# Second attention: the last two key tiles of exponentials summed on DVE instead of PE

## Chip, core and metric

The kernel runs on one core of a Trainium2 chip. The metric is the device time of one execution in microseconds (us); of several executions the median counts.

## What is computed

A convolutional attention, then a token attention, then routed experts, on eight images of 256 channels and 32x32 = 1024 tokens. The change lies in the token attention (the second attention):

```python
qk = jnp.einsum('bhqd,bhkd->bhqk', q, k)
qe = jnp.einsum('bhqd,qkd->bhqk', q, embeddings)
weights = jax.nn.softmax((qk + qe) / jnp.sqrt(jnp.float32(d_head)), axis=-1)
output = jnp.einsum('bhqk,bhkd->bhqd', weights, v)
```

There are 8 heads of 32 channels. The kernel computes the softmax as exponentials, a product of the unnormalized exponentials with the values, and a division by the sum of the exponentials (the denominator).

## The kernel before

The second attention is `attention_keys_first`. One **unit** of its work is one image, one group of four heads and one half (512) of the queries: 8 x 2 x 2 = 32 units. Keys lie on the partitions, so a unit has `KTU` = 8 **tiles** of 128 keys, and a tile has four exponential blocks of 128x512 f32, one for each head. The exponentials of the last `PR` = 4 tiles are kept in the ring `prob`. `prob`, the running sums `acc`, the reciprocals `rec` (and in the changed kernel `pair`) all are slices of one buffer that the trace calls `bias`.

The order of work is written out by hand: a loop over n = 8u + kt on each engine. I call the passage for one n a **step**, and number the steps of a unit 0 to 7 by `n % KTU`.

- **PE**, step n: the scores of heads 0 and 1 of tile n (`scores`, L1264), two products of a later unit's search for row extremes (`maxima`, L1145), the scores of heads 2 and 3, then `weigh(n-1)` (L1284), the product of tile n-1's exponentials with the values. Score s may start when exponential s-2 has been made (two PSUM buffers). The two products of `maxima` have one PSUM buffer each; each may start when DVE has read what stood in its buffer (`max_read`).
- **ACT**, step n: four exponentials (L1338), one a head. Before the first of a tile it waits until the ring's place is free: until tile n-4 has been weighed (`weighed`) and summed (`acc_ok`). In step 1 it also copies the unit's output from PSUM (L1323).
- **POOL** sums tiles 0 to 5 of a unit into `acc`: `ADDS` = 5 instructions of 128x2048 f32 (L1366), each after all four exponentials of its tile. After the fourth it normalizes the unit before (`finish`, L1349 and L1353), which needs that unit's four reciprocals, and then it makes the fifth sum.
- **DVE**, step n: reads the two products of `maxima` (L1153, 128x1024 from PSUM, 1 out); in steps 3 to 6 also one of the four reciprocals (L1381) of the unit before.
- **Denominators.** PE multiplies by a matrix of ones (`den_w`) and accumulates three groups of four matmuls in `den_ps`: the exponentials of tile 6 and of tile 7, each straight from `prob`, behind their `weigh` (L1293, in step 7 and in step 0 of the next unit), and Pool's sum `acc` in step 2 of the next unit (`denominators`, L1300).

Of the kernel before, what the change touches and what calls it, by code (L numbers as in the profile page):

```python
# [6 lines left out]
def build(nc, x, gamma, wqkv, wout, w1q, b1cols, b1v, gatew, experts, relt, cw0, cb0, cw1, cb1, cw2, cb2,  # L7
# [3 lines left out]
    ALU = mybir.AluOpType  # L11
# [7 lines left out]
    H, D = 8, C // 8  # L19
    G = H * D // P  # L20
    HG = H // G
# [9 lines left out]
    CH = 512  # L31
# [22 lines left out]
    with ctx:  # L54
# [1003 lines left out]
        def attention_keys_first():  # L1058
            with ExitStack() as es:
# [3 lines left out]
                def tile(name, shape, dt):  # L1063
                    return es.enter_context(nc.sbuf_tensor(f"{name}_kf", shape, dt))
# [11 lines left out]
                prob = zf[:, 0:o1].rearrange("p (r j n) -> p r j n", r=PR, j=HG)  # L1076
                acc = zf[:, o1:o2].rearrange("p (r j n) -> p r j n", r=2, j=HG)
                rec = zf[:, o2:o2 + 2 * CH].rearrange("p (r n) -> p r n", r=2)
                oS = tile("oS", [P, 2, CH], F32)
                oN = tile("oN", [P, CH], F32)  # L1080
                den_w = tile("den_w", [P, D], F32)
# [17 lines left out]

                sems = [ssem(n) for n in ("stk0", "stk1", "v_in0", "v_in1", "x_in0", "x_in1", "out_st0", "out_st1", "m_in0",  # L1100
                                          "m_in1", "emb_in", "fill", "max_full", "max_read", "full", "exps", "weighed",
                                          "acc_ok", "den", "recd", "taken", "scaled", "fin")]
                (stk0, stk1, v_in0, v_in1, x_in0, x_in1, out_st0, out_st1, m_in0, m_in1, emb_in, fill, max_full, max_read,
                 full, exps, weighed, acc_ok, den, recd, taken, scaled, fin) = sems
                stk, v_in, x_in, out_st, m_in = (stk0, stk1), (v_in0, v_in1), (x_in0, x_in1), (out_st0, out_st1), (m_in0, m_in1)

                def load_group(sp, q, b, g):
# [110 lines left out]
                with nc.Fori(0, B // NB) as i_:  # L1218
                    with nc.Block() as block:
# [35 lines left out]
                        def _(pe):  # L1255
# [19 lines left out]
                            def weigh(n):  # L1275
                                u, kt = divmod(n, KTU)
                                g, bb = (u // NC) % G, u // UB
                                if kt == 0 and u % UB == 0 and bb >= 1:
                                    pe.wait_ge(v_in[bb % 2], 16 * ((bb + 1) // 2))
                                if kt == 0 and u >= 1:  # L1280
                                    pe.wait_ge(taken, u)
                                pe.wait_ge(exps, HG * (n + 1))
                                for j in range(HG):
                                    last = nc.tensor.matmul(out_ps[j * D:(j + 1) * D, :],  # L1284
                                                            V[:, bb % 2, kt, (g * HG + j) * D:(g * HG + j + 1) * D],
                                                            prob[:, n % PR, j, :], start=(kt == 0), stop=(kt == KTU - 1),
                                                            skip_group_check=True)
                                if kt > ADDS:

                                    if kt == ADDS + 1 and u >= 1:  # L1290
                                        pe.wait_ge(recd, PIECES * u)
                                    for j in range(HG):
                                        last = nc.tensor.matmul(den_ps[j * D:(j + 1) * D, :], den_w[:], prob[:, n % PR, j, :],  # L1293
                                                                start=(kt == ADDS + 1), stop=False, skip_group_check=True)
                                last.then_inc(weighed, 1)

                            def denominators(u):
                                pe.wait_ge(acc_ok, ADDS * (u + 1))
                                for j in range(HG):
                                    last = nc.tensor.matmul(den_ps[j * D:(j + 1) * D, :], den_w[:], acc[:, u % 2, j, :],  # L1300
                                                            start=False, stop=True, skip_group_check=True)
                                last.then_inc(den, 1)

                            for n in range(NU * KTU + DEN + 1):
# [12 lines left out]
                        def _(act):  # L1317
# [7 lines left out]
                            for s in range(NS_ + SU):  # L1325
# [5 lines left out]
                                if n >= PR and j == 0:  # L1331

                                    u, kt = divmod(n - PR, KTU)
                                    act.wait_ge(weighed, n - PR + 1)
                                    if kt <= ADDS:
                                        act.wait_ge(acc_ok, ADDS * u + max(kt, 1))
                                act.wait_ge(full, s + 1)
                                nc.scalar.activation(prob[:, n % PR, j, :], score_ps[s % 2], ACT.Exp,  # L1338
                                                     scale=-1.0 / (W1S * W1S)).then_inc(exps, 1)
# [35 lines left out]
                        def _(dve):  # L1375
                            def reciprocal(u, piece):
# [3 lines left out]
                                c = slice(piece * CH // PIECES, (piece + 1) * CH // PIECES)  # L1380
                                nc.vector.reciprocal(rec[:, u % 2, c], den_ps[:, c]).then_inc(recd, 1)  # L1381

                            for n in range(NU * KTU + REC + PIECES):
                                if n < NU * KTU:
                                    for u, m in step_jobs[n]:
                                        max_reduce(dve, job_at[(u, m)], u, m)
                                u, piece = n // KTU - 1, n % KTU - REC
                                if u >= 0 and 0 <= piece < PIECES:
                                    reciprocal(u, piece)
# [503 lines left out]
```

## Time and profile before

| | us |
|---|---|
| median of 3 runs | 2957.65 |
| lowest, highest | 2957.21, 2963.11 |
| profiled execution, its own time | 2944.62 |
| its span in the trace | 2942.8 |
| busy PE, DVE, POOL, ACT | 2554.9, 2020.5, 1972.1, 1399.7 |
| matmuls of the second attention's scores (L1264), busy | 531.8 |
| Pool's sums of the second attention (L1366), busy | 724.8 |

The span is what the trace covers; the profiled execution's own time is 1.8 us longer and is one of the shorter ones seen. Busy times of PE count overlapping matmuls once for each stretch, so neighbouring groups of matmuls are best read by the distance between their starts. A time line row gives the start, the length of the merged group, the engine, the line, and in brackets how long the engine was idle before it and what released it.

### The profile page before, as it was taken

Reading aid. Unit: us, or ns where it says so; the run is one execution under the profiler, and the core shown is the slowest. Engines: PE = TensorE matmul, PEld = TensorE weight load, DVE = VectorE, ACT = ScalarE, POOL = GpSimd, SP = SyncE. Lnnn points to the kernel's source line nnn. Section 1 sums busy time; section 2 is a strip of 40 time slices with the busy share of each in tenths; the row PEclk is TensorE's granted clock in tenths of the full one; section 3 lists DMA queues with packets and bytes.
Section 4 is the critical chain, followed back from the end, with each engine's and each line's share of the span. In section 5 each row is a group of like instructions: output and inputs, shape, how many; then the busy total and the mean of one; then the engine's idle time right before and its main releaser. Section 6 shows DMA issues by size and latency. Waiting matters only on the chain. (4 is left out here: it accounts for less than half of the span.)

```text
span 2942.8 us, 47730 instructions
## 1 busy us (share of the span) xinstructions
PE 2554.9 (87%) x18726; PEld 871.1 (30%) x18726; DVE 2020.5 (69%) x3094; ACT 1399.7 (48%) x2549; POOL 1972.1 (67%) x767
## 2 busy tenths in 40 slices
PE   5669999999999999969998999999999999870355
PEld 1436222222222222225553222222222222250235
DVE  3346678787787878757776777777777777668224
ACT  3224555556555555523224555555555555450012
POOL 0312688888888888864445888878888788750673
PEclk8789999999999999989999999999999999985558
DMA  2985232122312223229654233222232222180237
GB/s 51 214 228 180 69 77 61 52 48 52 86 48 51 48 62 76 51 95 285 232 203 138 48 81 75 61 48 62 79 76 62 47 62 72 36 259 0 83 120 257
DMA packets 239569, 289.44 MB, mean 98 GB/s; under 512 B 65014, under 2 KB 172790, under 8 KB 236006
## 3 DMA queue, kind: packets, MB, share of 16 engines
q1 hardware_dynamic: 196528, 259.08, 31.9%
q0 software_dynamic: 6144, 16.85, 1.8%
q10 hardware_dynamic: 36672, 10.45, 1.6%
q8 instruction: 148, 2.42, 0.4%
q14 instruction: 77, 0.63, 0.1%
HBM read 176.55 MB, written 111.57 MB: 98 GB/s over the span
## 5 line engine op out<-in xcount | busy, mean ns | idle before, releaser
L1018 POOL TENSOR_TENSOR room_af<-room_af 128x2048 f32<-128x2048 f32 x160 | 726.9, 4543 | 162.6 <-ACT room_af L990 148.9
L1366 POOL TENSOR_TENSOR bias<-bias 128x2048 f32<-128x2048 f32 x160 | 724.8, 4530 | 147.6 <-ACT bias L1338 133.6
L1153 DVE TENSOR_REDUCE row_min_kf<-PS 128x1 f32<-128x1024 f32 x532 | 627.5, 1220 | 265.8 <-PE PS L1145 264.3
L797 DVE CUSTOM_DVE_ANT_0 PS<-PS,bias 128x1024 f32<-128x1024 f32 x532 | 644.3, 1241 | 174.6 <-PE PS L785 148.3
L1338 ACT ACTIVATE bias<-PS 128x512 f32<-128x512 f32 x1024 | 557.0, 596 | 411.0 <-PE PS L1264 409.9
L990 ACT ACTIVATE room_af<-PS 128x512 f32<-128x512 f32 x1024 | 555.9, 594 | 398.0 <-PE PS L912 398.0
L1264 PE MATMUL PS<-stacks_kf 128*128 128x512 f16 x2048 | 531.8, 382 | 7.5 <-PEq L85 7.1
L905 PE MATMUL PS<-QS_af,KS_af 128*128 128x512 f16 x1024 | 334.1, 387 | 11.1 <-PEq L85 4.5
L1264 PEld LDWEIGHTS PS<-stacks_kf 128*128 128x128 f16 x2048 | 157.0, 97 | 446.8 <-ACT bias L1338 291.6
L938 PE MATMUL PS<-room_af,V_af 128*32 128x512 f32 x2048 | 272.7, 605 | 0.3 <-ACT room_af L990 0.3
L1284 PE MATMUL PS<-bias,V_kf 128*32 128x512 f32 x2048 | 272.7, 604 | 0.0
L912 PE MATMUL PS<-turned_bias,eyes 64*32 64x512 f16 x4096 | 210.6, 388 | 0.0
L785 PE MATMUL PS<-KM_af,QM_af 32*128 32x512 f16 x1064 | 133.9, 386 | 52.5 <-DVE row_min_af L797 32.8
L1145 PE MATMUL PS<-stacks_kf 64*128 64x512 f16 x1064 | 168.8, 383 | 1.6
L905 PEld LDWEIGHTS PS<-QS_af,KS_af 128*128 128x128 f16 x1024 | 70.7, 97 | 306.0 <-ACT room_af L990 231.0
L1693 POOL DMA_INDIRECT G_t<-token_rows,idxT_t x64 | 65.9, 1029 | 109.5 <-DVE valT_t L1808 90.3
L577 POOL TENSOR_TENSOR room_af<-room_af 128x1024 f16<-128x1024 f32 x16 | 34.0, 2126 | 149.8 <-ACT room_af L535 149.7
L1381 DVE RECIPROCAL bias<-PS 128x128 f32<-128x128 f32 x128 | 121.0, 947 | 6.0 <-PE PS L1300 6.0
L470 PE MATMUL PS<-xh,w_p 128*128 128x512 f16 x384 | 124.4, 383 | 0.0
L1037 DVE RECIPROCAL room_af<-room_af 128x128 f32<-128x128 f32 x128 | 121.1, 948 | 1.1
L1664 ACT CAST gh_t<-PS 128x256 f16<-128x256 f32 x64 | 23.8, 373 | 202.4 <-PE PS L1594 202.1
L912 PEld LDWEIGHTS PS<-turned_bias,eyes 64*32 64x32 f16 x4096 | 57.4, 89 | 186.3 <-issue 186.3
(179 smaller groups left out, 2844.7 us busy)
## 6 DMA issues: line engine op xcount, KB each, us to landing
stacks_kf<-query_key_halves SPq DMA_DIRECT2D x119, 256.0 KB, 7.2
query_key_halves<-bias SPq DMA_DIRECT2D x32, 768.0 KB, 3.8
query_key_halves<-room_af SPq DMA_DIRECT2D x32, 512.0 KB, 3.0
KS_af<-query_key_halves SPq DMA_DIRECT2D x51, 256.0 KB, 4.8
QS_af<-query_key_halves SPq DMA_DIRECT2D x51, 256.0 KB, 7.0
V_kf<-values SPq DMA_DIRECT2D x9, 1024.0 KB, 10.8
V_af<-values SPq DMA_DIRECT2D x17, 512.0 KB, 8.8
stacks_kf<-query_key_halves SPq DMA_DIRECT2D x68, 128.0 KB, 9.4
```

Of the source, the lines that this page charges most:

```text
L797: nc.vector.tensor_tensor_reduce(out=max_ps[n % len(max_ps)], in0=max_ps[n % len(max_ps)], in1=bias[:, g * HG + j, z:z + N], scale=-1.0, s ...
L905: nc.tensor.matmul(score_ps[s % 3], KS[:, g, j, kt * P:(kt + 1) * P], QS_[:, g, j, first:first + CH], start=True, stop=False, skip_group_c ...
L912: last = nc.tensor.matmul(score_ps[(HG * n + 2 * pair + i) % 3][c * W:(c + 1) * W, :], eyes[half, :], turned_bias[half, 2 * g + pair, z:z ...
L938: last = nc.tensor.matmul(out_ps[j * D:(j + 1) * D, :], V[:, q % 2, kt, j * D:(j + 1) * D], prob[:, n % PR, j, :], start=(kt == 0), stop=( ...
L990: nc.scalar.activation(prob[:, n % PR, head, :], score_ps[s % 3], ACT.Exp).then_inc(exps, 1)
L1018: nc.gpsimd.tensor_tensor(acc[:, u % 2], so_far, prob[:, n % PR], ALU.add).then_inc(acc_ok, 1)
L1145: last = nc.tensor.matmul(max_ps[n % len(max_ps)][:, c * CH:(c + 1) * CH], stacks[half, slot, QHH, j, first + t * P:first + (t + 1) * P], ...
L1153: nc.vector.tensor_reduce(row_min[:, m:m + 1], max_ps[n % len(max_ps)], AX.X, ALU.min).then_inc(max_read, 1)
L1264: last = nc.tensor.matmul(score_ps[s % 2], stacks[:, slot, k_, j, kt * P:(kt + 1) * P], stacks[:, slot, q_, j, first:first + CH], start=(n ...
L1284: last = nc.tensor.matmul(out_ps[j * D:(j + 1) * D, :], V[:, bb % 2, kt, (g * HG + j) * D:(g * HG + j + 1) * D], prob[:, n % PR, j, :], st ...
L1338: nc.scalar.activation(prob[:, n % PR, j, :], score_ps[s % 2], ACT.Exp, scale=-1.0 / (W1S * W1S)).then_inc(exps, 1)
L1366: nc.gpsimd.tensor_tensor(acc[:, u % 2], so_far, prob[:, n % PR], ALU.add).then_inc(acc_ok, 1)
```

## The change

PE no longer multiplies tiles 6 and 7 by `den_w` one after the other. DVE adds the two tiles, head by head, into a new buffer `pair`: four `tensor_tensor` instructions of 128x512 f32 (`add_pair`), two in step 0 and two in step 1 of the next unit, each behind one of the two reads of `maxima` in that step. `denominators`, still in step 2 of the next unit, now issues two groups of four matmuls, one from `pair` and one from `acc`. PE waits there for `paired`, for `acc_ok` and for the reciprocals of the unit before. ACT, before it writes over tiles 6 and 7 in the ring (at the start of steps 2 and 3 of the next unit), now waits for `paired` too.

```diff
--- before.py
+++ after.py
@@ -1076,6 +1076,7 @@
                 prob = zf[:, 0:o1].rearrange("p (r j n) -> p r j n", r=PR, j=HG)
                 acc = zf[:, o1:o2].rearrange("p (r j n) -> p r j n", r=2, j=HG)
                 rec = zf[:, o2:o2 + 2 * CH].rearrange("p (r n) -> p r n", r=2)
+                pair = zf[:, o2 + 2 * CH:o2 + 6 * CH].rearrange("p (j n) -> p j n", j=HG)
                 oS = tile("oS", [P, 2, CH], F32)
                 oN = tile("oN", [P, CH], F32)
                 den_w = tile("den_w", [P, D], F32)
@@ -1099,9 +1100,9 @@
 
                 sems = [ssem(n) for n in ("stk0", "stk1", "v_in0", "v_in1", "x_in0", "x_in1", "out_st0", "out_st1", "m_in0",
                                           "m_in1", "emb_in", "fill", "max_full", "max_read", "full", "exps", "weighed",
-                                          "acc_ok", "den", "recd", "taken", "scaled", "fin")]
+                                          "acc_ok", "paired", "den", "recd", "taken", "scaled", "fin")]
                 (stk0, stk1, v_in0, v_in1, x_in0, x_in1, out_st0, out_st1, m_in0, m_in1, emb_in, fill, max_full, max_read,
-                 full, exps, weighed, acc_ok, den, recd, taken, scaled, fin) = sems
+                 full, exps, weighed, acc_ok, paired, den, recd, taken, scaled, fin) = sems
                 stk, v_in, x_in, out_st, m_in = (stk0, stk1), (v_in0, v_in1), (x_in0, x_in1), (out_st0, out_st1), (m_in0, m_in1)
 
                 def load_group(sp, q, b, g):
@@ -1285,20 +1286,17 @@
                                                             V[:, bb % 2, kt, (g * HG + j) * D:(g * HG + j + 1) * D],
                                                             prob[:, n % PR, j, :], start=(kt == 0), stop=(kt == KTU - 1),
                                                             skip_group_check=True)
-                                if kt > ADDS:
-
-                                    if kt == ADDS + 1 and u >= 1:
-                                        pe.wait_ge(recd, PIECES * u)
+                                last.then_inc(weighed, 1)
+
+                            def denominators(u):
+                                if u >= 1:
+                                    pe.wait_ge(recd, PIECES * u)
+                                pe.wait_ge(paired, HG * (u + 1))
+                                pe.wait_ge(acc_ok, ADDS * (u + 1))
+                                for i, part in enumerate((pair, acc[:, u % 2])):
                                     for j in range(HG):
-                                        last = nc.tensor.matmul(den_ps[j * D:(j + 1) * D, :], den_w[:], prob[:, n % PR, j, :],
-                                                                start=(kt == ADDS + 1), stop=False, skip_group_check=True)
-                                last.then_inc(weighed, 1)
-
-                            def denominators(u):
-                                pe.wait_ge(acc_ok, ADDS * (u + 1))
-                                for j in range(HG):
-                                    last = nc.tensor.matmul(den_ps[j * D:(j + 1) * D, :], den_w[:], acc[:, u % 2, j, :],
-                                                            start=False, stop=True, skip_group_check=True)
+                                        last = nc.tensor.matmul(den_ps[j * D:(j + 1) * D, :], den_w[:], part[:, j, :],
+                                                                start=(i == 0), stop=(i == 1), skip_group_check=True)
                                 last.then_inc(den, 1)
 
                             for n in range(NU * KTU + DEN + 1):
@@ -1334,6 +1332,8 @@
                                     act.wait_ge(weighed, n - PR + 1)
                                     if kt <= ADDS:
                                         act.wait_ge(acc_ok, ADDS * u + max(kt, 1))
+                                    else:
+                                        act.wait_ge(paired, HG * (u + 1))
                                 act.wait_ge(full, s + 1)
                                 nc.scalar.activation(prob[:, n % PR, j, :], score_ps[s % 2], ACT.Exp,
                                                      scale=-1.0 / (W1S * W1S)).then_inc(exps, 1)
@@ -1380,10 +1380,24 @@
                                 c = slice(piece * CH // PIECES, (piece + 1) * CH // PIECES)
                                 nc.vector.reciprocal(rec[:, u % 2, c], den_ps[:, c]).then_inc(recd, 1)
 
+                            def add_pair(u, j):
+                                dve.wait_ge(exps, HG * KTU * (u + 1))
+                                if u >= 1:
+                                    dve.wait_ge(den, u)
+                                last = KTU * (u + 1) - 1
+                                nc.vector.tensor_tensor(pair[:, j, :], prob[:, (last - 1) % PR, j, :], prob[:, last % PR, j, :],
+                                                        ALU.add).then_inc(paired, 1)
+
                             for n in range(NU * KTU + REC + PIECES):
+                                u, kt = n // KTU - 1, n % KTU
+                                heads = [2 * kt, 2 * kt + 1] if u >= 0 and kt < HG // 2 else []
                                 if n < NU * KTU:
-                                    for u, m in step_jobs[n]:
-                                        max_reduce(dve, job_at[(u, m)], u, m)
+                                    for u_, m in step_jobs[n]:
+                                        max_reduce(dve, job_at[(u_, m)], u_, m)
+                                        if heads and m < MH:
+                                            add_pair(u, heads.pop(0))
+                                for j in heads:
+                                    add_pair(u, j)
                                 u, piece = n // KTU - 1, n % KTU - REC
                                 if u >= 0 and 0 <= piece < PIECES:
                                     reciprocal(u, piece)
```

How it moves the instructions. On **DVE**, from step 6 of a unit (the row of L1155 or L1156 is the transposed extremes) to the first reciprocal of the next unit, before:

```order
L1155 TENSOR_SCALAR max_row_kf<-PS 16x128 [waits max_full_kf]
L1153 TENSOR_REDUCE row_min_kf<-PS 128x1 [waits max_full_kf] x2
L1381 RECIPROCAL bias<-PS 128x128 [waits den_kf]
L1153 TENSOR_REDUCE row_min_kf<-PS 128x1 [waits max_full_kf] x10
L1381 RECIPROCAL bias<-PS 128x128 [waits den_kf]
L1153 TENSOR_REDUCE row_min_kf<-PS 128x1 [waits max_full_kf] x2
L1381 RECIPROCAL bias<-PS 128x128 [waits den_kf]
L1153 TENSOR_REDUCE row_min_kf<-PS 128x1 [waits max_full_kf] x2
L1381 RECIPROCAL bias<-PS 128x128 [waits den_kf]
```

and now, from the same place (L1388 is `add_pair`; `bias` is the common buffer):

```order
L1156 TENSOR_SCALAR max_row_kf<-PS 16x128 [waits max_full_kf]
L1154 TENSOR_REDUCE row_min_kf<-PS 128x1 [waits max_full_kf] x2
L1381 RECIPROCAL bias<-PS 128x128 [waits den_kf]
L1154 TENSOR_REDUCE row_min_kf<-PS 128x1 [waits max_full_kf] x3
L1388 TENSOR_TENSOR bias<-bias 128x512 [waits den_kf,exps_kf]
L1154 TENSOR_REDUCE row_min_kf<-PS 128x1 [waits max_full_kf]
L1388 TENSOR_TENSOR bias<-bias 128x512 [waits den_kf,exps_kf]
L1154 TENSOR_REDUCE row_min_kf<-PS 128x1 [waits max_full_kf]
L1388 TENSOR_TENSOR bias<-bias 128x512 [waits den_kf,exps_kf]
L1154 TENSOR_REDUCE row_min_kf<-PS 128x1 [waits max_full_kf]
L1388 TENSOR_TENSOR bias<-bias 128x512 [waits den_kf,exps_kf]
L1154 TENSOR_REDUCE row_min_kf<-PS 128x1 [waits max_full_kf] x4
```

Four additions stand between five reads; they wait for the exponentials and, for the buffer `pair`, for the denominators of the unit before. No other DVE instruction of the second attention has changed its place.

On **PE**, the end of step 2, where `denominators` stands behind `weigh`, before:

```order
L1284 MATMUL PS<-bias,V_kf 32x512 [waits exps_kf]
L1284 MATMUL PS<-bias,V_kf 32x512 x3
L1300 MATMUL PS<-bias,den_w_kf 32x512 [waits acc_ok_kf]
L1300 MATMUL PS<-bias,den_w_kf 32x512 x3
L1264 MATMUL PS<-stacks_kf 128x512 [waits exps_kf]
```

and now:

```order
L1285 MATMUL PS<-bias,V_kf 32x512 [waits exps_kf]
L1285 MATMUL PS<-bias,V_kf 32x512 x3
L1298 MATMUL PS<-bias,den_w_kf 32x512 [waits acc_ok_kf,paired_kf,recd_kf]
L1298 MATMUL PS<-bias,den_w_kf 32x512 x7
L1265 MATMUL PS<-stacks_kf 128x512 [waits exps_kf]
```

The group of four has become eight, with two more waits; the groups of L1293 in steps 7 and 0 are gone.

On **ACT**, from the middle of step 1 into step 2, before:

```order
L1338 ACTIVATE bias<-PS 128x512 [waits full_kf,acc_ok_kf,weighed_kf]
L1338 ACTIVATE bias<-PS 128x512 [waits full_kf]
L1323 COPY oS_kf<-PS 128x512 [waits weighed_kf]
L1338 ACTIVATE bias<-PS 128x512 [waits full_kf] x2
L1338 ACTIVATE bias<-PS 128x512 [waits full_kf,weighed_kf]
L1338 ACTIVATE bias<-PS 128x512 [waits full_kf] x3
```

and now:

```order
L1338 ACTIVATE bias<-PS 128x512 [waits full_kf,acc_ok_kf,weighed_kf]
L1338 ACTIVATE bias<-PS 128x512 [waits full_kf]
L1321 COPY oS_kf<-PS 128x512 [waits weighed_kf]
L1338 ACTIVATE bias<-PS 128x512 [waits full_kf] x2
L1338 ACTIVATE bias<-PS 128x512 [waits full_kf,paired_kf,weighed_kf]
L1338 ACTIVATE bias<-PS 128x512 [waits full_kf] x3
```

The first exponential of step 2 has one more wait, `paired_kf`; so has that of step 3.

## Rows read from the trace of the kernel before

**Rows 1.** The page: span, and busy time of each engine.

```profile
span 2942.8 us, 47730 instructions
...
PE 2554.9 (87%) x18726; PEld 871.1 (30%) x18726; DVE 2020.5 (69%) x3094; ACT 1399.7 (48%) x2549; POOL 1972.1 (67%) x767
```

**Rows 2.** Windows: us, then busy PE, PEld, DVE, ACT, POOL, clock, DMA share, GB/s.

```profile
1620.00:2540.00 920.00, 918.41 (x5548) 240.39 (x5548) 677.54 (x630) 532.38 (x990) 753.90 (x210) 1.00 0.26 64
```

**Rows 3.** Groups by line: busy us, mean ns of one, idle before and its releaser.

```profile
L1366 POOL TENSOR_TENSOR bias<-bias 128x2048 f32<-128x2048 f32 x160 | 724.8, 4530 | 147.6 <-ACT bias L1338 133.6 <-POOL bias L1366 0.4
...
L1153 DVE TENSOR_REDUCE row_min_kf<-PS 128x1 f32<-128x1024 f32 x532 | 627.5, 1220 | 265.8 <-PE PS L1145 264.3
...
L1264 PE MATMUL PS<-stacks_kf 128*128 128x512 f16 x2048 | 531.8, 382 | 7.5 <-PEq L85 7.1 <-ACT bias L1338 0.3
...
L1284 PE MATMUL PS<-bias,V_kf 128*32 128x512 f32 x2048 | 272.7, 604 | 0.0
...
L1293 PE MATMUL PS<-bias,den_w_kf 128*32 128x512 f32 x512 | 66.6, 592 | 0.0
...
L1300 PE MATMUL PS<-bias,den_w_kf 128*32 128x512 f32 x256 | 33.7, 597 | 2.2 <-POOL bias L1366 2.2
```

**Rows 4.** Time line of one unit of the second attention (step 0 starts at 1729.62).

```profile
1698.32 4.53 POOL L1366 TENSOR_TENSOR bias<-bias 128x2048 f32<-128x2048 f32 x1
...
1721.48 1.04 PE L1264 MATMUL PS<-stacks_kf 128*128 128x512 f16 x4
...
1726.36 1.27 POOL L1349 TENSOR_TENSOR oN_kf<-oS_kf,bias 128x512 f32<-128x512 f32 x1 [1.19 <-DVE bias L1381]
...
1729.00 4.53 POOL L1366 TENSOR_TENSOR bias<-bias 128x2048 f32<-128x2048 f32 x1
...
1729.62 1.04 PE L1264 MATMUL PS<-stacks_kf 128*128 128x512 f16 x4
...
1731.02 2.35 DVE L1153 TENSOR_REDUCE row_min_kf<-PS 128x1 f32<-128x1024 f32 x2 [1.97 <-PE PS L1145]
...
1733.95 1.04 PE L1264 MATMUL PS<-stacks_kf 128*128 128x512 f16 x4
...
1734.67 1.08 ACT L1338 ACTIVATE bias<-PS 128x512 f32<-128x512 f32 x2 [1.82 <-PE PS L1264]
...
1734.92 0.60 PE L1145 MATMUL PS<-stacks_kf 64*128 64x512 f16 x4
...
1735.46 1.04 PE L1264 MATMUL PS<-stacks_kf 128*128 128x512 f16 x4
...
1736.11 1.12 ACT L1338 ACTIVATE bias<-PS 128x512 f32<-128x512 f32 x2
...
1737.30 4.54 POOL L1366 TENSOR_TENSOR bias<-bias 128x2048 f32<-128x2048 f32 x1 [3.77 <-ACT bias L1338]
...
1737.42 1.04 PE L1264 MATMUL PS<-stacks_kf 128*128 128x512 f16 x4
```

**Rows 5.** The line L1748 alone: shortest, median and longest in ns.

```profile
L1748 DVE TENSOR_SCALAR gates<-lg_t x16: 180/559/1094, 2590.2 to 2643.8; 128x32 f32<-128x32 f32 x16
```

**Rows 6.** Time line of the expert stage, where L1748 meets Pool's L1687.

```profile
2603.82 2.27 POOL L1687 TENSOR_TENSOR xl_t<-bias,xh_t 128x512 f16<-128x512 f32 x2 [1.69 <-ACT xh_t L1634]
...
2604.02 1.00 DVE L1748 TENSOR_SCALAR gates<-lg_t 128x32 f32<-128x32 f32 x1
...
2604.93 0.68 DVE L1755 SCALAR_TENSOR_TENSOR bias<-PS,bias 128x512 f16<-128x512 f32 x1
...
2622.34 0.18 DVE L1748 TENSOR_SCALAR gates<-lg_t 128x32 f32<-128x32 f32 x1
...
2622.49 2.27 POOL L1687 TENSOR_TENSOR xl_t<-bias,xh_t 128x512 f16<-128x512 f32 x2 [1.74 <-ACT xh_t L1634]
```

**Rows 7.** DVE groups by form, f32 from SBUF to SBUF: two inputs, one input.

```profile
L1775 DVE TENSOR_TENSOR gates<-gates,rcp_t 128x512 f32<-128x512 f32 x8 | 5.5, 692 | 0.3
...
L252 DVE TENSOR_SCALAR set_weights<-set_weights 128x768 f32<-128x768 f32 x2 | 1.1, 602 | 0.0
```

More of the change, by code:

```diff
@@ L1287, in weigh @@
                                                             skip_group_check=True)
-                                if kt > ADDS:
-                                    if kt == ADDS + 1 and u >= 1:
-                                        pe.wait_ge(recd, PIECES * u)
-                                    for j in range(HG):
-                                        last = nc.tensor.matmul(den_ps[j * D:(j + 1) * D, :], den_w[:], prob[:, n % PR, j, :],
-                                                                start=(kt == ADDS + 1), stop=False, skip_group_check=True)
                                 last.then_inc(weighed, 1)
                             def denominators(u):
+                                if u >= 1:
+                                    pe.wait_ge(recd, PIECES * u)
+                                pe.wait_ge(paired, HG * (u + 1))
                                 pe.wait_ge(acc_ok, ADDS * (u + 1))
-                                for j in range(HG):
-                                    last = nc.tensor.matmul(den_ps[j * D:(j + 1) * D, :], den_w[:], acc[:, u % 2, j, :],
-                                                            start=False, stop=True, skip_group_check=True)
+                                for i, part in enumerate((pair, acc[:, u % 2])):
+                                    for j in range(HG):
+                                        last = nc.tensor.matmul(den_ps[j * D:(j + 1) * D, :], den_w[:], part[:, j, :],
+                                                                start=(i == 0), stop=(i == 1), skip_group_check=True)
                                 last.then_inc(den, 1)
```

## The prediction

> **What bounds the kernel now.** I read the page first, for the engine that is busiest, then the windows of the second attention, then its groups by line, and last one unit of it in the time line. PE is busy 2554.9 of 2942.8 us [rows 1], and between 1620 and 2540 us it is busy 918.4 of 920 us at a granted clock of 1.00, so at its upper level of 2.4 GHz [rows 2]. DVE is busy 677.5 us there and POOL 753.9. By shares, then, PE is the bound, and DVE has 242 us to spare. The groups say the same: before the scores (L1264) PE has idled 7.5 us in all, and Pool has held PE back by 2.2 us at L1300; DVE waits 264.3 us for products, and Pool 133.6 us for exponentials [rows 3].
>
> The share does not say what a unit's chain of waits tolerates; that needs the time line [rows 4]. Step 0 starts at 1729.62, step 1 at 1733.95, step 2 at 1737.42: a step with a denominator group takes 4.33 us, one without 3.47, so a group of four matmuls costs 0.86 us. A unit takes 30.68 us (Pool's fifth sum starts at 1698.32 and 1729.00). Counted from the start of a step: the first product of L1145 starts at 0.97, the third score at 1.51 (so the second product at about 1.24), the first exponential at 0.72 and the last one ends at 3.28, DVE's two reads start at 1.40 and take 1.18 each.
>
> Two things are nearer to PE than its 99.8% shows. Pool's fifth sum ends at 1733.53, and ACT, which must wait for it before the exponentials of step 1, starts them at 1734.67: 1.1 us of slack. And two exponentials are made in 1.08 us; the first of them ends 1.26 us into a step, 0.25 us before the third score that waits for it starts. A late exponential reaches PE after about 0.15 us (0.25 less some 0.1 for the signal, my estimate).
>
> **What the change takes away.** Two groups before (steps 7 and 0), one more in step 2: one group of 0.86 us a unit, 32 x 0.86 = 27.5 us, all of it on PE. Steps 7 and 0 shrink to 3.47, step 2 grows from 4.33 to 5.2. A unit would take 29.82 us if nothing else held it.
>
> **What it adds.** Four additions a unit on DVE, 128x512 f32, two inputs in SBUF. The same form took 692 ns in the routing [rows 7], 0.65 from start to start if successive instructions overlap by 0.04 as the reads do (1220 ns each, 1.18 apart). That is 4 x 0.65 x 32 = 83 us, which DVE's spare time covers by share. What matters is when they run, and beside what.
>
> *When.* All times now count from step 0. Pool's fifth sum hangs on the reciprocals of step 6: it starts 7.52 us after step 6 does (1721.48, [rows 4]), through `finish`, which waited for DVE 1.19 us. Step 0 used to come 8.14 us after step 6, now 7.28. So the sum runs from 0.24 to 4.77, while the exponentials of step 1 are due at 3.47 + 0.72 = 4.19: the slack of 1.1 us has turned into 0.6 late. With additions that nothing hinders, DVE does read 1.40 to 2.58, addition to 3.23, read to 4.41, addition to 5.06, and in step 1 read, addition, read, addition to 8.72. ACT now waits for that last addition before step 2's exponentials, due at 6.94 + 0.72 = 7.66. So they are 1.1 late, PE loses 0.95 (this contains the 0.6), and a unit takes 29.82 + 0.95 = 30.8 instead of 30.68. Even undisturbed, the whole gain is given back.
>
> *Beside what.* The trace shows that some DVE instructions and Pool's exclude each other. L1748, a DVE instruction of 32 elements, takes between 180 and 1094 ns, median 559 [rows 5]. At 2622.34 no Pool instruction runs yet: 0.18 us. At 2604.02 the first of two Pool subtractions (2603.82, 2.27 us for both, so the first ends near 2604.97) is under way: 1.00 us, ending at 2605.02, so it waited out that instruction and got in ahead of the second one [rows 6]. The neighbour that reads PSUM (L1755) took its 0.68 with Pool beside it, and the 532 reads of L1153 average 1220 ns under Pool's sums. L1748 has one input, in SBUF; the rows show that such f32 instructions go at double rate (768 elements in 602 ns, where two inputs need 692 for 512, [rows 7]), hence through two read paths. An addition of two SBUF tensors needs two read paths as well, so I take it that it too waits for a Pool instruction under way, and holds up the next. No row shows a two-input addition beside Pool; that is the open step. The bounds are 0.65 for an addition (nothing held) and 4.53 + 0.65 = 5.2 (a whole sum of L1366 waited for, [rows 3]).
>
> The Trainium skill, "SBUF — State Buffer", section "Who interferes with whom", says that a DVE instruction with two SBUF inputs contends with a GpSimd instruction that reads SBUF, and that the pair of ports goes to whoever starts first, for the whole instruction. By that rule the additions behave as I assume; without it the sum would be the 30.8 us above. The trace agrees for the one-input form (0.18 against 1.00 us), and shows neither for the two-input one.
>
> **The sum with exclusion.** DVE's first addition is ready at 2.58, Pool's sum runs until 4.77: it ends at 5.42, the second read at 6.60. PE's second product of step 1, due at 3.47 + 1.24 = 4.71, waits for that buffer: **1.9 us lost**, queued behind it the two later scores. The second addition finds Pool idle and ends at 7.25, the read at 8.43. The exponentials of tile 1 end at 3.47 + 3.28 + 1.9 = 8.65, and Pool's first sum could start at 8.72; the third addition is there 0.3 us earlier and takes 8.43 to 9.08. Pool's sum runs 9.08 to 13.61. DVE's read ends at 10.26, and the fourth addition waits for Pool: 13.61 to 14.26. ACT may start step 2's exponentials at 14.3, where 6.94 + 0.72 + 1.9 = 9.56 was due: 4.75 late, **4.6 us lost** on PE (a product of step 2 that waits until 10.26 is inside that). From there Pool has nothing that meets an addition, the reciprocals keep their place, and the next fifth sum again ends 4.77 after step 0. A unit takes 29.82 + 6.5 = 36.3 us, 5.6 more than 30.68. Over the 31 units behind the first: 175 us. The last unit pays some 2 us (its additions meet the last sum; one group less on PE). Together 177: the profiled execution's 2944.6 would become 3122. The median of the runs shown is 13 us above that execution, so I give 2957.65 + 177 = **3135**.
>
> **The rivals.**
> - *Pool gets in first.* The lead of the third addition is only 0.3 us. If Pool's first sum starts at 8.72, the additions end at 13.90 and 15.73, step 2 loses 6.05 and a unit 7.95 + 29.82 = 37.8: 7.1 more, 222 in all, **3180**. For it: the lead is small beside signals that I estimate at 0.1. Against it: the chain from the second read runs over PE, ACT (two exponentials, 1.12) and Pool, against an addition and a read, 1.83 us.
> - *Sharing instead of exclusion.* If the two only slow each other (additions twice as long beside Pool, the sum longer by 0.65), the fourth ends near 10.1, ACT is 2.5 late, a unit takes 1.5 more: +47, **3005**. Against it: in rows 6 the short instruction ended with Pool's, not after a share of it.
> - *Nothing held: the two-input form is not affected.* 30.8 a unit, +3 to +5: **2961**, within 0.2%, which is about what a measurement here can tell from no change. For it: only the one-input form is seen waiting.
> - *Faster.* Neither wait binds: PE takes the full 27.5 us, **2930**. It needs the fourth addition done by about 7.8, so additions of 0.43 us, and nothing held. A form that takes 692 ns speaks against it; it turns into a gain over 0.2% once an unhindered unit loses under 0.65 us of the 0.86 instead of 0.95, which exponentials with 0.3 us more slack would give.
>
> **How the numbers follow.** Forecast 0.58, Pool first 0.22, sharing 0.07, nothing held 0.09, faster 0.04. The forecast's own ends: if a held addition has read its inputs before and ends 0.25 after Pool instead of 0.65, two of them give back 0.8 us a unit, 25 us: 3110; signals of 0.2 where I took 0.1 add 10. With Pool first and the same allowance the upper end is 3195, the lower one 3100; this leaves out the last three cases, 0.20. Slower holds 0.58 + 0.22 + 0.07 and a sliver of "nothing held": 0.88; within 0.2%, 0.08; faster 0.04.
>
> **What would show it.** Right: the first and fourth additions of a unit last about 2.9 and 4 us and start while L1366 runs, the second and third about 0.7; L1145 and the exponentials of step 2 gain idle time released by DVE, some 2 and 5 us a unit; units 36.3 us apart; PE's busy share of the stage falls to about 82% at a clock that stays 1.00; the groups before and behind the stage are unchanged. Pool first: the third addition is long as well. Wrong: four additions of 0.7 us each beside L1366, and units of 30.8 us. A granted clock below 1.00 in the stage would add time that I have not counted.

## The result and the profile after

| | before | after |
|---|---|---|
| median, us | 2957.43 | 3170.22 |
| lowest to highest, us | 2956.62 to 2963.11 | 3167.54 to 3175.49 |
| profiled execution, its own time | 2944.62 | 3175.49 |

The changed kernel is slower: ratio 1.0717, 95% interval 1.0698 to 1.0736, 213 us. The forecast was 3135, the range 3100 to 3195.

The page of the kernel after, span and busy times, to be read against [rows 1]:

```profile
span 3173.7 us, 47502 instructions
...
PE 2594.9 (82%) x18470; PEld 875.8 (28%) x18470; DVE 2260.6 (71%) x3222; ACT 1402.9 (44%) x2549; POOL 1971.6 (62%) x767
```

PE is busy 40 us more, although its matmul instructions are 256 fewer (18470 against 18726); DVE is busy 240 us more, where four additions a unit, unhindered, are 83. The windows after, of the second attention and of two stretches of one of its units (columns as in [rows 2]):

```profile
1620.00:2740.00 1120.00, 950.31 (x5288) 242.11 (x5288) 894.06 (x746) 534.34 (x987) 749.07 (x209) 0.95 0.21 52
...
1772.90:1775.70 2.80, 2.76 (x12) 0.63 (x16) 1.57 (x2) 1.61 (x3) 0.91 (x1) 0.67 0.00 0
1775.70:1778.30 2.60, 2.60 (x20) 0.52 (x12) 0.00 (x0) 0.00 (x0) 2.60 (x1) 0.70 0.00 0
```

Before, PE was busy 99.8% of the stage at a clock of 1.00; now it is busy 84.8% at 0.95. The groups by line after (lines 1145, 1264 and 1284 of before are now 1146, 1265 and 1285; against [rows 3]):

```profile
L1338 ACT ACTIVATE bias<-PS 128x512 f32<-128x512 f32 x1024 | 557.0, 595 | 619.5 <-PE PS L1265 407.9 <-DVE bias L1388 161.9 <-POOL bias L1366 49.5
...
L1265 PE MATMUL PS<-stacks_kf 128*128 128x512 f16 x2048 | 536.2, 384 | 133.4 <-ACT bias L1338 126.2 <-PEq L85 7.1
...
L1388 DVE TENSOR_TENSOR bias<-bias 128x512 f32<-128x512 f32 x128 | 252.1, 1972 | 0.0
...
L1146 PE MATMUL PS<-stacks_kf 64*128 64x512 f16 x1064 | 174.1, 384 | 52.0 <-DVE row_min_kf L1154 50.3
```

L1265 has idled 133.4 us where it was 7.5, nearly all of it for exponentials; L1146, the products for the extremes, 52.0 us for DVE's reads. ACT in turn waited 161.9 us for the additions and 49.5 for Pool. The additions alone (shortest, median, longest in ns):

```profile
L1388 DVE TENSOR_TENSOR bias<-bias x128: 672/683/4983, 1611.0 to 2778.4; 128x512 f32<-128x512 f32 x128
```

Half of them take 0.68 us, the longest 5 us, and their mean is 1972 ns. The time line of one unit shows which (against [rows 4]):

```profile
1758.51 1.04 PE L1265 MATMUL PS<-stacks_kf 128*128 128x512 f16 x4
1758.76 4.52 POOL L1366 TENSOR_TENSOR bias<-bias 128x2048 f32<-128x2048 f32 x1
...
1761.05 2.78 DVE L1388 TENSOR_TENSOR bias<-bias 128x512 f32<-128x512 f32 x1
...
1761.98 1.04 PE L1265 MATMUL PS<-stacks_kf 128*128 128x512 f16 x4
...
1764.89 0.67 DVE L1388 TENSOR_TENSOR bias<-bias 128x512 f32<-128x512 f32 x1
...
1765.02 0.39 PE L1146 MATMUL PS<-stacks_kf 64*128 64x512 f16 x2 [1.68 <-DVE row_min_kf L1154]
...
1766.62 0.67 DVE L1388 TENSOR_TENSOR bias<-bias 128x512 f32<-128x512 f32 x1
1767.15 4.51 POOL L1366 TENSOR_TENSOR bias<-bias 128x2048 f32<-128x2048 f32 x1 [3.87 <-ACT bias L1338]
...
1767.31 1.04 PE L1265 MATMUL PS<-stacks_kf 128*128 128x512 f16 x4
...
1768.36 3.85 DVE L1388 TENSOR_TENSOR bias<-bias 128x512 f32<-128x512 f32 x1
...
1772.29 1.08 ACT L1338 ACTIVATE bias<-PS 128x512 f32<-128x512 f32 x2 [5.22 <-DVE bias L1388]
...
1772.94 1.14 PE L1265 MATMUL PS<-stacks_kf 128*128 128x512 f16 x4 [4.06 <-ACT bias L1338]
...
1778.32 1.04 PE L1265 MATMUL PS<-stacks_kf 128*128 128x512 f16 x4
...
1796.02 1.04 PE L1265 MATMUL PS<-stacks_kf 128*128 128x512 f16 x4
```

Step 0 starts at 1758.51. The first addition starts at 1761.05, while Pool's fifth sum runs (1758.76 to 1763.28), and ends at 1763.83; the second takes 0.67. The second product of step 1 waits 1.68 us for a read behind them. The third addition comes 0.53 us before Pool's first sum; the fourth starts 1.2 us into that sum (1767.15 to 1771.66) and ends at 1772.21. ACT starts step 2's exponentials at 1772.29, and PE, idle for 4.06 us, takes up the third score at 1772.94. From there to step 3 it needs 5.38 us, where the schedule has 3.47 - 1.51 + 2 x 0.86 = 3.68: the windows above show a granted clock of 0.67 and 0.70, that is, part of the time at 1.2 GHz.

The unit's account: step 1 lasts 5.33 us instead of 3.47 (**1.86 lost**); the third score of step 2 comes 5.63 us into the step instead of 1.51 (**4.12 lost**); the rest of step 2 takes 5.38 instead of 3.68 (**1.70 lost, the clock**). 29.82 + 7.68 = 37.5, which is what lies between 1758.51 and 1796.02. Over 30 units the mean is 37.56, against 30.70 before; 31 x 6.86 = 213 us, the whole difference. Nothing outside the second attention is needed to explain it. (The two profiled executions differ by more, 231 us. Of these, 212 lie between the first and the last row of L1155/L1156, 2 ahead of it and 16 behind it. From that last row to the end of the trace before takes 391 us and after 408; the other traces below take 393 to 411 there, and the kernel before with nothing but Pool's order changed takes 402. So the 16 us are the spread of that stage from one execution to the next, and not the change.)

### The profile page after: what moved, and what is told of

Read it like the earlier page. It is cut to its first block and busy times, and to the rows that moved or that the text cites. A ratio compares the mean times of both kernels' runs of the same rounds, so it can differ in the third digit from the quotient of the medians.

```text
span 3173.7 us, 47502 instructions
## 1 busy us (share of the span) xinstructions
PE 2594.9 (82%) x18470; PEld 875.8 (28%) x18470; DVE 2260.6 (71%) x3222; ACT 1402.9 (44%) x2549; POOL 1971.6 (62%) x767
## 5 line engine op out<-in xcount | busy, mean ns | idle before, releaser
L1265 PE MATMUL PS<-stacks_kf 128*128 128x512 f16 x2048 | 536.2, 384 | 133.4 <-ACT bias L1338 126.2
L1265 PEld LDWEIGHTS PS<-stacks_kf 128*128 128x128 f16 x2048 | 155.2, 97 | 568.0 <-ACT bias L1338 424.9
L1285 PE MATMUL PS<-bias,V_kf 128*32 128x512 f32 x2048 | 299.5, 660 | 0.0
L1388 DVE TENSOR_TENSOR bias<-bias 128x512 f32<-128x512 f32 x128 | 252.1, 1972 | 0.0
L1146 PE MATMUL PS<-stacks_kf 64*128 64x512 f16 x1064 | 174.1, 384 | 52.0 <-DVE row_min_kf L1154 50.3
L1622 PE MATMUL PS<-bias,gh_t 128*128 128x256 f16 x256 | 62.6, 344 | 88.9 <-DVE gl_t L1831 68.4
```

The costliest lines, as they stand in the source:

```text
L1265: last = nc.tensor.matmul(score_ps[s % 2], stacks[:, slot, k_, j, kt * P:(kt + 1) * P], stacks[:, slot, q_, j, first:first + CH], start=(n ...
L1285: last = nc.tensor.matmul(out_ps[j * D:(j + 1) * D, :], V[:, bb % 2, kt, (g * HG + j) * D:(g * HG + j + 1) * D], prob[:, n % PR, j, :], st ...
L1388: nc.vector.tensor_tensor(pair[:, j, :], prob[:, (last - 1) % PR, j, :], prob[:, last % PR, j, :], ALU.add).then_inc(paired, 1)
```

## The experiments

All ratios are against the kernel before, timed on the same chip beside them (2947.18 us for the first four, 2962.81 for the next four, 2958.73 for the last three). "Unit" is the mean distance between the rows of L1155/L1156, over 30 units of the trace.

**One operand from PSUM.** 

```diff
+ other = den_ps if u >= 1 else prob[:, last % PR, j, :]
- nc.vector.tensor_tensor(pair[:, j, :], prob[:, (last - 1) % PR, j, :], prob[:, last % PR, j, :], ALU.add)
+ nc.vector.tensor_tensor(pair[:, j, :], prob[:, (last - 1) % PR, j, :], other, ALU.min)
```

> The addition of each head takes its second operand from PSUM (the denominators' bank) and not from SBUF, as a minimum; place, length and waits stay, the sum over tile 7 is left out. Theory (an instruction of DVE with two SBUF inputs and one of Pool's exclude each other): nothing is held, all four last about 0.7 us, a unit takes 30.8 us, time about 2961. Rival (any DVE instruction that reads the buffer that Pool reads is held): first and fourth still last 2.8 and 3.9 us, time stays near 3170.

2952.16 us, ratio 1.0018 (1.0008 to 1.0027), unit 30.61. Its lines of the additions:

```profile
L1389 DVE TENSOR_TENSOR bias<-bias,PS x124: 674/677/682, 1645.7 to 2563.3; 128x512 f32<-128x512 f32 x124
L1389 DVE TENSOR_TENSOR bias<-bias x4: 681/683/4130, 1610.0 to 1615.2; 128x512 f32<-128x512 f32 x4
```

124 additions with one operand in PSUM stand at the same places, beside the same sums of Pool, read the same buffer, and take 674 to 682 ns. The four of the first unit, which kept both operands in SBUF, include one of 4130 ns. So what is held is the instruction with a second SBUF input; the buffer and the place do not matter. (The minimum is not what frees it either: the one of 4130 ns is a minimum too.) The run also confirms that the change, with nothing held, gives nearly its whole gain back: 0.77 of 0.86 us a unit (30.61 against 29.84 in the last run). The 5 us by which the kernel is slower than before are about what its first unit, with that one held addition, takes more than the others (35.69 against 30.60).

**One column.** 

```diff
- pair[:, j, :], prob[:, (last - 1) % PR, j, :], prob[:, last % PR, j, :]
+ pair[:, j, 0:1], prob[:, (last - 1) % PR, j, 0:1], prob[:, last % PR, j, 0:1]
```

> Each addition covers 1 column instead of 512; it still has two SBUF inputs, and all waits stay (the denominators leave out nearly all of tiles 6 and 7). Theory: what costs is the waiting, not the adding. The first still ends with Pool's fifth sum (4.9 us after step 0 starts), the fourth with Pool's first sum (near 12.8). PE loses 1.35 and 3.65 us and 0 to 1.7 us for the clock: units of 34.8 to 36.5 us, time 3085 to 3140. Rival (the 2.7 us of added DVE work hold up the reads): without the work a unit takes 30.3 us, time about 2946.

3158.50 us, ratio 1.0715 (1.0696 to 1.0733), unit 37.50: as slow as the change, and above what I expected. From its time line:

```profile
1791.69 2.25 DVE L1388 TENSOR_TENSOR bias<-bias 128x1 f32<-128x1 f32 x1
...
1797.26 4.50 POOL L1366 TENSOR_TENSOR bias<-bias 128x2048 f32<-128x2048 f32 x1 [3.34 <-ACT bias L1338]
1797.40 4.37 DVE L1388 TENSOR_TENSOR bias<-bias 128x1 f32<-128x1 f32 x1
...
1802.51 1.89 PE L1265 MATMUL PS<-stacks_kf 128*128 128x512 f16 x4 [3.51 <-ACT bias L1338]
...
1808.98 1.04 PE L1265 MATMUL PS<-stacks_kf 128*128 128x512 f16 x4
```

An addition of one column, 0.14 us where it is free, takes 2.25 and 4.37 us: the work is not what costs. PE's idle time fell as expected (1.15 us in step 1, 3.51 in step 2). But from the third score at 1802.51 to step 3 PE took 6.47 us instead of 3.68, and the windows of that stretch (columns as in [rows 2]) show the lower clock all through its first part:

```profile
1802.50:1806.00 3.50, 3.49 (x12) 0.79 (x16) 1.54 (x2) 1.64 (x3) 0.89 (x1) 0.50 0.75 143
1806.00:1808.90 2.90, 2.90 (x20) 0.59 (x12) 0.00 (x0) 0.00 (x0) 2.90 (x1) 0.60 0.00 0
```

So the clock took 2.8 us here and not the 0 to 1.7 I had allowed. That left a question, for the last series.

**No additions.** `add_pair` and the waits for `paired` go; both groups in `denominators` multiply `acc`, so tiles 6 and 7 are left out of the denominators and PE's work stays.

> No additions on DVE and no waits for them; PE multiplies Pool's sum twice, so its two groups of four stay (the denominators leave out tiles 6 and 7). It gives what PE's saved group is worth at best. If PE alone bounds: 29.82 us a unit, time 2930. By my reading of the slack, Pool's fifth sum is now 0.6 us late for step 1's exponentials and takes back 0.5: 30.3 us a unit, time about 2946. In no case above 2957.

2939.74 us, ratio 0.9974 (0.9962 to 0.9986), unit 30.42, where I expected 30.3. Waits of this kernel from 1700 to 2400 us (total, times, longest):

```profile
ACT bias L1335 <- POOL bias L1363: 37.1, 23, 1.6
```

ACT waits 1.6 us a unit for Pool's fifth sum, and the best that the rest of the change could bring as it stands is 7.4 us (2947.18 - 2939.74).

**Pool's sums in halves.** 

```diff
- nc.gpsimd.tensor_tensor(acc[:, u % 2], so_far, prob[:, n % PR], ALU.add).then_inc(acc_ok, 1)
+ for h in range(2):
+     hs = slice(h * HG // 2, (h + 1) * HG // 2)
+     nc.gpsimd.tensor_tensor(acc[:, u % 2, hs], so_far[:, hs], prob[:, n % PR, hs], ALU.add).then_inc(acc_ok, 1)
```

Everyone who waits for `acc_ok` waits for twice the count.

> Pool makes each sum in two instructions of 128x1024 (about 2.35 us each) instead of one of 128x2048. Theory (DVE is held until the Pool instruction under way ends, and then gets in before the next one): no addition is held for longer than 2.3 us, the fourth ends near 11 us after step 0 starts instead of 13.7; PE loses some 3.2 us a unit: 33.0 us, time about 3030, up to 3070 if the clock still falls. Rivals: if two Pool instructions in a row keep the ports, or if the hold is not tied to an instruction's end, the time stays at 3170 or rises, since Pool has 0.15 us more work a sum.

3057.97 us, ratio 1.0367 (1.0347 to 1.0387), unit 34.14, where I expected 33.0 and up to 3070 us if the clock still falls. Time line of Pool's pairs of halves and the two held additions:

```profile
1815.46 5.18 POOL L1368 TENSOR_TENSOR bias<-bias 128x1024 f32<-128x1024 f32 x2
...
1819.48 1.71 DVE L1390 TENSOR_TENSOR bias<-bias 128x512 f32<-128x512 f32 x1
...
1823.35 5.10 POOL L1368 TENSOR_TENSOR bias<-bias 128x1024 f32<-128x1024 f32 x2 [2.71 <-ACT bias L1338]
...
1823.98 2.26 DVE L1390 TENSOR_TENSOR bias<-bias 128x512 f32<-128x512 f32 x1
...
1828.78 4.67 POOL L1368 TENSOR_TENSOR bias<-bias 128x1024 f32<-128x1024 f32 x2 [0.33 <-ACT bias L1338]
```

An undisturbed pair takes 4.67 us; the two pairs with an addition inside take 5.18 and 5.10. The held additions, the second and the fourth of this unit, last 1.71 and 2.26 us, where the change had 2.78 and 3.85. Of the pair at 1823.35 the first half ends at 1825.69, the addition at 1826.24 and the second half at 1828.45. So the hold ends with Pool's instruction, DVE gets in ahead of the next one though that is ready, and then Pool waits for DVE: the exclusion works both ways. The units of this run are not alike: most are near 33.2, 33.9 or 34.8 us. In those of 33.2 PE goes from the third score of step 2 to step 3 in 3.74 us, in those of 34.8 in 5.2 to 5.4; from 1640 to 2500 us the granted clock is 0.97 on average. So part of what lies above the expected 33.0 is again the lower clock.

**Filling PE's wait.** In step 2 of the changed kernel, before the third score:

```diff
+ pe.wait_ge(acc_ok, ADDS * (ud + 1))
+ for _ in range(4):
+     for j in range(HG):
+         nc.tensor.matmul(den_ps[j * D:(j + 1) * D, :], den_w[:], acc[:, ud % 2, j, :], start=True, stop=True, ...)
```

(`ud` is the unit before; a wait for its predecessor's reciprocals is left out here.)

> In step 2, behind the products for the extremes, PE issues four groups of four extra matmuls (the ones matrix by Pool's sum, into the denominators' bank, written over afterwards): 3.45 us of useless work in the 4.06 us in which it otherwise waits for the fourth addition. All waits stay. If the lower granted clock behind that wait costs 1.7 us a unit, a unit falls from 37.5 to 35.8 us: some 52 us less than the change, 160 above before, although PE has 110 us more to do. If the clock is not the cause, the time is that of the change (210 above before) or more.

3132.18 us, ratio 1.0573 (1.0557 to 1.0589), unit 35.92. The window of its stage (columns as in [rows 2]) and the time line of its step 2 (L1314 is the useless work; the trace has two records for one f32 matmul, so x32 are 16 matmuls):

```profile
1640.00:2500.00 860.00, 805.58 (x5007) 210.09 (x5006) 720.53 (x599) 427.21 (x790) 602.05 (x168) 1.00 0.22 55
...
1798.32 3.89 DVE L1397 TENSOR_TENSOR bias<-bias 128x512 f32<-128x512 f32 x1
...
1798.78 3.64 PE L1314 MATMUL PS<-bias,den_w_kf 128*32 128x512 f32 x32
...
1802.95 1.09 PE L1265 MATMUL PS<-stacks_kf 128*128 128x512 f16 x4 [0.53 <-ACT bias L1347]
...
1806.69 1.04 PE L1265 MATMUL PS<-stacks_kf 128*128 128x512 f16 x4
```

The fourth addition is as long as before and ACT resumes as late, yet from the third score to step 3 PE takes 3.74 us and not 5.38. 110 us of additional matmuls make the kernel 1.3% faster (1.0573 against 1.0717), and the granted clock of the stage is 1.00 where the change had 0.95. This shows the 1.7 us a unit to be the clock's.

**Pool's fifth sum first.** Two lines in Pool's loop:

```diff
- if n % KTU == FIN and n >= KTU:
+ if n % KTU == ADDS and n >= KTU:
      finish(n // KTU - 1)
```

(and `finish` waits for the previous `fin`, since two of them now follow one another at the end).

> Pool makes its fifth sum before it normalizes the unit before, not after; the additions stay where they are. The fifth sum then ends 0.6 us before step 0 starts, the normalizing about 2 us after, so Pool is free when the first addition comes (2.6 us): the first, second and third last 0.7 us, PE's loss of 1.9 us in step 1 goes. The fourth still meets Pool's first sum, now from 6.9 to 11.4 us, and ends near 12.0: 4.25 us lost in step 2 and 1.7 for the clock. Unit 34.1 to 35.8 us, 105 to 160 above before. If the loss in step 1 is not Pool's doing, 210 above.

3128.26 us, ratio 1.0560 (1.0543 to 1.0576), unit 36.06. Time line:

```profile
1787.36 1.26 POOL L1355 TENSOR_TENSOR res_kf<-res_kf,oN_kf 128x512 f32<-128x512 f32 x1
...
1789.05 0.68 DVE L1390 TENSOR_TENSOR bias<-bias 128x512 f32<-128x512 f32 x1
...
1792.52 0.68 DVE L1390 TENSOR_TENSOR bias<-bias 128x512 f32<-128x512 f32 x1
...
1793.34 4.50 POOL L1368 TENSOR_TENSOR bias<-bias 128x2048 f32<-128x2048 f32 x1 [4.72 <-ACT bias L1338]
...
1794.25 4.13 DVE L1390 TENSOR_TENSOR bias<-bias 128x512 f32<-128x512 f32 x1
...
1799.12 1.89 PE L1265 MATMUL PS<-stacks_kf 128*128 128x512 f16 x4 [4.09 <-ACT bias L1338]
```

Pool's normalizing ends at 1788.6, the first addition is at 1789.05: three additions of 0.68 (two shown), no loss in step 1. The fourth, 0.9 us behind the start of Pool's first sum, still takes 4.13. The time is a little above what I expected: the wait in step 2 was as expected (4.09 us idle, the third score 4.16 late), which leaves 36.06 - 29.82 - 4.16 = 2.1 us a unit, on average, for the clock. It is not the same in every unit: most are 35.3 and 36.4 us long in turn, behind the same wait. The granted clock from 1640 to 2500 us is 0.93.

**Fifth sum first, and all four additions in step 0.** One before the first read, one behind it, two behind the second:

```diff
- heads = [2 * kt, 2 * kt + 1] if u >= 0 and kt < HG // 2 else []
+ heads = list(range(HG)) if u >= 0 and kt == 0 else []
+ if heads:
+     add_pair(u, heads.pop(0))
```

> As with the fifth sum first, and all four additions stand in step 0: one before the first read, one behind it, two behind the second. All meet only the short normalizing instructions of Pool (1.3 us each) and end near 5.7 us, a microsecond before Pool's first sum can start; the reads end at 8.1 us, in time for step 2. Nothing holds PE: 29.85 us a unit, 26 us below before (0.991). Rival (the DVE work itself delays the reads, or the waits bind anyhow): no gain, 30.7 us or more a unit.

2944.27 us against 2962.81, ratio 0.9930 (0.9917 to 0.9944), unit 30.07 (29.85 expected): **faster than both kernels**, by little, but the whole interval lies below 1. Time line of its step 0 (1789.94) and 1:

```profile
1790.08 1.27 POOL L1351 TENSOR_TENSOR oN_kf<-oS_kf,bias 128x512 f32<-128x512 f32 x1
1790.15 1.75 DVE L1390 TENSOR_TENSOR bias<-bias 128x512 f32<-128x512 f32 x1
...
1791.49 1.54 POOL L1355 TENSOR_TENSOR res_kf<-res_kf,oN_kf 128x512 f32<-128x512 f32 x1
...
1792.96 0.68 DVE L1390 TENSOR_TENSOR bias<-bias 128x512 f32<-128x512 f32 x1
...
1794.39 0.82 PE L1146 MATMUL PS<-stacks_kf 64*128 64x512 f16 x4
1794.69 1.28 DVE L1390 TENSOR_TENSOR bias<-bias 128x512 f32<-128x512 f32 x2
...
1796.95 23.21 POOL L1368 TENSOR_TENSOR bias<-bias 128x2048 f32<-128x2048 f32 x5 [3.92 <-ACT bias L1338]
```

The additions meet only Pool's two normalizing instructions: the first waits for one (1.75 us), and then holds up the other (1.54 instead of 1.28). All four are done at 1795.97, a microsecond before Pool's first sum. The third score of step 1 follows 1.72 us after the step's start (1793.42) instead of 1.51; these 0.21 us are nearly all that lies between 30.07 and the unit of 29.84 that PE's work alone takes (last run).

**The same, but no addition before the first read** (the last two lines of the edit above left out).

> As the run before, but no addition stands before the first read of step 0: one behind the first read, three behind the second and so at the end of step 0. They end near 6.35 us, just ahead of Pool's first sum at 6.8, but the reads of step 1 end 0.5 us later than step 2 wants them: 30.3 to 30.4 us a unit, 9 us below before (0.997). If the fourth misses by half a microsecond and meets Pool's sum, it costs 4 us a unit: 120 above.

2949.46 us, ratio 0.9953 (0.9940 to 0.9967), unit 30.19: also faster than before, its unit 0.1 us longer than the last one's, where I had expected 0.5.

**One column, and the wait filled.** The edits of one column and of filling together (leaving out what the first of them leaves out).

> Additions of one column, and PE fills its wait in step 2 with the four useless groups (3.45 us of the 3.5 it waits). The run with one column alone was as slow as the change (37.53 us a unit) although the fourth addition ended 1.1 us sooner; its trace shows the lower granted clock for 6 us a unit where the change has 3.4. If that is the reason, the clock now stays up and a unit takes what its waits say, 29.82 + 1.33 (step 1) + 3.6 (step 2) = 34.75 us: 126 above before (1.043). If something else ate the gain, 210 above (1.071).

3093.58 us, ratio 1.0454 (1.0437 to 1.0471), unit 34.84. The window of its stage:

```profile
1620.00:2640.00 1020.00, 985.12 (x6137) 255.02 (x6133) 847.87 (x730) 521.30 (x964) 736.56 (x205) 1.00 0.23 57
```

With useless work in the wait the granted clock is 1.00, and the unit is what its waits say. So one column did save 1.1 us of waiting a unit (34.84 against 35.92 with whole additions and the wait filled), and the clock had taken it.

**The kernel before with the fifth sum first.**

> The kernel before, with nothing but Pool's fifth sum made ahead of the normalizing. Pool held nothing up there, so a unit stays at 30.68 us: no difference (1.000). If Pool's order is worth something alone, the gain of the four early additions is not the additions': 0.993.

2958.31 us, ratio 0.9998 (0.9988 to 1.0007), unit 30.70. Pool's order is worth nothing by itself; it only makes room.

**No additions, fifth sum first.** Without the additions, as above.

> No additions and no waits for them, and Pool's fifth sum ahead of the normalizing. The run without additions took 30.41 us a unit where PE's work alone is 29.82; ACT waited for Pool there. If the fifth sum is what is missing, a unit now takes 29.82 us, 27 us below before (0.991). If not, it stays at 30.4 (0.997).

2927.18 us, ratio 0.9888 (0.9872 to 0.9905), unit 29.84. That is PE's own work, 29.82 by the sum.

## Why the prediction was right, and where it was off

The way, the cause and the size of the two waits were right. That the time lies in the range is in part luck: the forecast's own ends were 3110 and 3145, and 3170 is inside only because the range was drawn up to 3195 for Pool coming first, which did not happen.

- *PE's group is worth 0.86 us a unit.* Right: 30.70 - 29.84 where nothing else binds.
- *Pool's fifth sum becomes late by 0.6 us.* Right: without additions a unit took 30.42, and 29.84 with the sum made earlier.
- *Unhindered additions give the gain back: 30.8 us a unit.* Right in kind, 30.61 measured; the signals cost less than I took.
- *Two SBUF inputs and Pool's instruction exclude each other.* This was the open step, inferred from an instruction with one input at double rate [rows 5 to 7]. It held: 2.78 and 3.85 us where I had 2.84 and 4.0, and 0.68 with one operand in PSUM. The Trainium skill ("SBUF — State Buffer", "Who interferes with whom") had the rule for two inputs, and for the PSUM case that an instruction with one SBUF input does not contend (outside DVE's two-port modes); these runs agree with both, 0.68 us against up to 4 us. It speaks of a hold for the whole instruction; Pool's halves agree, since the hold shrank with the instruction.
- *The third addition gets in ahead of Pool's sum.* Right, by 0.53 us where I had 0.3. The rival in which Pool came first, whose 3180 lies nearer to the measured time than my 3135, did not happen: the third addition takes 0.67. A time alone would have chosen the wrong case.
- *PE loses 1.9 and 4.6 us.* 1.86 and 4.12 measured. The fourth addition ended 0.55 us behind Pool's sum, not 0.65, and Pool's sum started 0.4 us sooner, 8.64 us into the unit and not 9.08: I had it wait for the end of the third addition at 9.08, but that ends at 8.78, and the row of Pool's sum starts 0.14 us before that end and is no longer than others (4.51 us).
- *"At a clock that stays 1.00."* This is the step that failed. I took PE's wait of more than 4 us as a wait only. Behind it the granted clock fell, and the matmuls that followed took 1.70 us longer; filling the wait took that away. PE's busy share of the stage fell to 84.8% and not to 82%, because matmuls at the lower clock keep PE busy for longer. I had named a lower clock as time not counted, and put it at nothing without a reason. Without the clock the account is 29.82 + 5.98 = 35.80 us a unit, 5.1 above before, 158 us (I had 177); the clock's 1.70 x 31 = 53 us brings it to 211. A term of 19 us too much and one of 53 missing make 34 of the 36 us between 177 and 213.

What stays open: why the lower clock lasts longer in some kernels than in others behind a wait of nearly the same length (2.8 us lost behind 3.51 with one column, 1.7 behind 4.06 in the change), and why it lasts longer in some units than in others of one kernel, behind the same wait (Pool's fifth sum first). The change and the one-column kernel settle at the same distance, 37.5 us a unit, though their waits differ by 1.1; no run here shows whether that is chance. Equal times do not mean equal waits.

## What to carry to other kernels

Before work is moved to DVE because its busy share leaves room, count how many SBUF tensors the new instruction reads and lay its place beside Pool's instructions: here 0.68 us of work became 2.8 and 3.9. If it can't take an operand from PSUM, put it where Pool is idle or runs short instructions; making one long sum of Pool earlier and putting all four additions into step 0 turned 7% slower into 0.7% faster. And price a wait of PE by what follows it, too: the matmuls behind a wait of 4 us may run at the lower clock.

## What the runs showed of the hardware that I had not expected

Useless matmuls can pay: 16 more a unit in a wait that was there anyway saved 1.64 us a unit (37.56 to 35.92). And a shorter wait need not be faster: one-column additions cut PE's idle time by 1.1 us a unit and changed the unit by 0.06 (37.50 against 37.56), until the clock was kept up, when it took 34.84.
